# Feed-forward gate of a gated cross-attention block: product and maximum in one instruction, four buffers of gate integers

## The reference, cut to what matters

```
def act_qdq(x):                                  # one scale for the whole tensor
    scale = max(max(|x|) / 32767, 1e-12)
    return clip(round(x / scale), -32768, 32767) * scale
x    = act_qdq(layernorm(x))
up   = act_qdq(x @ Wup.T)                        # 2048 x 768
gate = act_qdq(x @ Wgate.T)                      # 2048 x 768
sig  = clip(round(sigmoid(gate) * 65536), 0, 65535) / 65536
gate = act_qdq(gate * sig)
o    = act_qdq(gate * up)
return o @ Wdown.T
```

## Time and profile before

| | us |
|---|---|
| median of 3 runs | 1151.55 (1150.32 to 1151.62) |
| the profiled execution | 1151.44 |
| its span in the trace | 1149.6 |
| DVE busy | 1006.2 (88%) |
| PE busy | 1075.3 (94%) |
| ACT busy | 604.5 (53%) |
| POOL busy | 37.0 (3%) |

### The profile page before, as it was taken

How to read it: one execution, slowest core, us unless ns; L and a number is a source line. 1 busy time by engine, 2 the same in 40 slices (tenths; PEclk the granted TensorE clock), 3 DMA queues, 4 the chain that set the end, 5 groups by cost and what they waited for, 6 DMA issues and landing times.

```text
span 1149.6 us, 20469 instructions
## 1 busy us (share of the span) xinstructions
PE 1075.3 (94%) x8342; PEld 501.4 (44%) x8342; DVE 1006.2 (88%) x1390; ACT 604.5 (53%) x706; POOL 37.0 (3%) x41
## 2 busy tenths in 40 slices
PE   5999999999999999999999999999999998999059
PEld 3443344434443444344434443444344323887049
DVE  7687988898989898999898989887999999749996
ACT  3555555555555555555555555554555464449652
POOL 0500000000000000000000000000000000003200
PEclk9999999999999999999999999999999999999579
DMA  8001300010001000100010001000000000000002
GB/s 264 18 20 25 120 20 20 20 38 20 20 20 37 20 20 20 38 20 19 21 38 20 20 20 38 20 20 20 30 20 19 20 29 10 1 1 1 0 0 74
DMA packets 37860, 34.57 MB, mean 30 GB/s; under 512 B 14209, under 2 KB 28738, under 8 KB 37510
## 3 DMA queue, kind: packets, MB, share of 16 engines
q1 hardware_dynamic: 37766, 33.26, 9.4%
HBM read 30.75 MB, written 2.36 MB: 29 GB/s over the span
## 4 chain that ended last, share of the span: by engine, by line
PE 80%; DVE 9%; ACT 5%; issue 5%; DMA 0%; POOL 0%; POOLq 0%; SPq 0%; DVEq 0%; ACTq 0%
PE ps L1384 26%; PE ps L1400 26%; PE ps L1247 5%; PE ps L1312 4%; PE ps L1257 4%; PE ps L1265 4%; PE ps L1534 3%; PE ps L1579 3%; DVE acc L925 2%; PE ps L1276 1%; DVE e_buf L1022 1%; DVE gt L1174 1%; ACT z L746 1%; ACT e_buf L664 1%; ACT z L748 1%
## 5 line engine op out<-in xcount | busy, mean ns | idle before, releaser
L664 ACT ACTIVATE e_buf<-ps 128x1024 f32<-128x1024 f32 x400 | 410.4, 1026 | 310.6 <-PE ps L1384 302.3
L1400 PE MATMUL ps<-e_buf,vb 64*64 64x512 f32 x3072 | 401.2, 593 | 4.7 <-DVE e_buf L1022 4.6
L925 DVE TENSOR_TENSOR acc<-acc,e_buf 128x1024 f32<-128x1024 f32 x318 | 387.8, 1220 | 0.0
L1022 DVE TENSOR_SCALAR e_buf<-e_buf 128x1024 f32<-128x1024 f32 x400 | 274.8, 687 | 53.9 <-ACT e_buf L664 52.6
L1384 PE MATMUL ps<-qb,kb_odd 64*64 64x512 f32 x1600 | 208.7, 589 | 0.0
L1384 PE MATMUL ps<-qb,kb_even 64*64 64x512 f32 x1600 | 208.6, 589 | 0.0
L1400 PEld LDWEIGHTS ps<-e_buf,vb 64*64 64x64 f32 x3072 | 111.7, 133 | 221.4 <-issue 187.4
L1384 PEld LDWEIGHTS ps<-qb,kb_odd 64*64 64x64 f32 x1600 | 61.5, 133 | 109.9 <-issue 109.6
L1384 PEld LDWEIGHTS ps<-qb,kb_even 64*64 64x64 f32 x1600 | 61.3, 133 | 110.2 <-issue 110.1
L1011 DVE TENSOR_TENSOR xacc<-ps,xacc 128x512 f32<-128x512 f32 x60 | 41.2, 690 | 35.4 <-PE ps L1312 34.9
L1534 PE MATMUL ps<-hT,wgu 128*128 128x512 f32 x288 | 67.7, 396 | 0.1
(11 more groups left out here) (151 smaller groups left out, 776.9 us busy)
## 6 DMA issues: line engine op xcount, KB each, us to landing
ebc<-el_rows SPq DMA_DIRECT2D x64, 128.0 KB, 2.9
rden<-inv_rows SPq DMA_DIRECT2D x62, 128.0 KB, 2.9
xacc<-in_x_dram SPq DMA_DIRECT2D x4, 512.0 KB, 7.2
wst<-in_L_xattn_Wkv_dram SPq DMA_DIRECT2D x16, 128.0 KB, 2.7
out_dram<-z SPq DMA_DIRECT2D x7, 256.0 KB, 2.5
wst<-in_L_xattn_Wq_dram SPq DMA_DIRECT2D x8, 128.0 KB, 2.7
wo_raw<-in_L_xattn_Wo_dram SPq DMA_DIRECT2D x8, 128.0 KB, 3.4
acc<-in_ctx_dram SPq DMA_DIRECT2D x2, 512.0 KB, 7.5
```

The lines of the kernel that those rows point to most:

```text
L664: nc.scalar.activation(e_buf[:, g % E_BUFS, :, :], sc[:, g % 2, :, :], ACT.Exp, scale=float(DH) ** -0.5).then_inc(exp_done, 1)
L925: dve.tensor_tensor(acc[:, t0 % 3, :, :], a, e_buf[:, tiles_to(t0, st) % E_BUFS, :, :], ALU.add).then_inc(summed, 1)
L1022: dve.tensor_scalar(tile, tile, EXP_LO, EXP_HI, ALU.max, ALU.min).then_inc(clip_done, 1)
L1400: ins = pe.matmul(ps_o[DH * h:DH * h + DH, half, :], vb[rows, p % 2, st, DH * h:DH * h + DH], e_buf[rows, g % E_BUFS, h, :], start=(st == ...
```

## The change

Each part by its line in the kernel before:

- The product (L1163) and its maximum (L809, `fst<-gt` in the product loop) become one instruction, `tensor_tensor_reduce`: it writes -(gi * su) over the chunk of `gt` and the largest of these values, with 0 as the start, to one column. The sign is turned, so the column holds the largest magnitude among the negative gates only. The last factor of the output (L1181) gets the sign back.
- The positive side comes from the largest gates, since x * sigmoid(x) grows with x there: DVE takes the plain maximum of each gate chunk (`gate_peak`, 12 reductions of 128 x 1024: ten in the gate phase, two between the first scale and the product loop). One column then goes through the same steps as the tensor: `peak_i` (DVE), sigmoid (ACT), `peak_u` (POOL), product (DVE in turn 2), all 128 x 1.
- `gi` has four buffers (`GI_BUFS`). In the product loop DVE makes eight of the twelve chunks of gate integers (0 and 1 ahead of the loop, 3, 4, 6, 7, 9 and 10 in it), ACT four (2, 5, 8, 11). ACT's order in a turn is now: sigmoid, two copies of up results, then perhaps `gi` of the next chunk.
- In the second product loop ACT's wait before `gi` is for the product four chunks back, not two.
- PE runs 12 matmuls on the identity, `keep_clock(7, 12)`, after the last up matmul.

The core of the diff:

```diff
@@ gpsimd, in the loop over su
+                if e == 1:
+                    pool.wait_ge(peak_sig, 1)
+                    pool.tensor_scalar(peak_u[:, :], peak[:, 1:2], U16, 1.0, ALU.mult, ALU.mult).then_inc(peak_su, 1)
@@ scalar
             for e in range(FCH):
-                f1_take(half + 2 * e)
-                f1_take(half + 2 * e + 1)
                 if e == 0:
                     act.wait_ge(scale_done, 2)
                     act.wait_ge(h_low, KT * NBS)
                 if e >= 2:
                     act.wait_ge(su_done, e - 1)
-                    act.wait_ge(gs_done, e - 1)
-
-                if e:
-                    nc.scalar.activation(gi[:, e % 2, :, :], chunk(gt, e), ACT.Copy, scale=fsc[:, 1, 2:3]).then_inc(gi_done, 1)
-                act.wait_ge(gi_done, e + 1)
-                nc.scalar.activation(sg[:, e % 2, :, :], gi[:, e % 2, :, :], ACT.Sigmoid, scale=fsc[:, 1, 1:2]).then_inc(sig_done, 1)
+                if gi_by_scalar(e):
+                    act.wait_ge(gi_scalar, e // 3 + 1)
+                else:
+                    act.wait_ge(gi_done, e - e // 3 + 1)
+                nc.scalar.activation(sg[:, e % 2, :, :], gi_at(e), ACT.Sigmoid, scale=fsc[:, 1, 1:2]).then_inc(sig_done, 1)
+                if e == 1:
+                    act.wait_ge(peak_gi, 1)
+                    nc.scalar.activation(peak[:, 1:2], peak_i[:, :], ACT.Sigmoid, scale=fsc[:, 1, 1:2]).then_inc(peak_sig, 1)
+                f1_take(half + 2 * e)
+                f1_take(half + 2 * e + 1)
+                if gi_by_scalar(e + 1) and e + 1 < FCH:
+                    if e + 1 >= GI_BUFS:
+                        act.wait_ge(gs_done, e + 2 - GI_BUFS)
+                    nc.scalar.activation(gi_at(e + 1), chunk(gt, e + 1), ACT.Copy,
+                                         scale=fsc[:, 1, 2:3]).then_inc(gi_scalar, 1)
             act.wait_ge(scale_done, 3)
             for e in range(FCH):
                 if e >= 2:
                     nc.scalar.activation(chunk(ui, e), chunk(up, e), ACT.Copy, scale=fsc[:, 2, 2:3]).then_inc(ui_done, 1)
-                    act.wait_ge(o_done, e - 1)
-                nc.scalar.activation(gi[:, e % 2, :, :], chunk(gt, e), ACT.Copy, scale=fsc[:, 3, 2:3]).then_inc(gq_done, 1)
+                if e >= GI_BUFS:
+                    act.wait_ge(o_done, e + 1 - GI_BUFS)
+                nc.scalar.activation(gi_at(e), chunk(gt, e), ACT.Copy, scale=fsc[:, 3, 2:3]).then_inc(gq_done, 1)
@@ vector
+            def gate_peak(e):
+                return dve.tensor_reduce(fst[:, 5, 2 * e:2 * e + 2], chunk(gt, e), AX_X, ALU.max)
+            def gate_integers(e):
+                if e >= GI_BUFS:
+                    dve.wait_ge(gs_done, e + 1 - GI_BUFS)
+                dve.tensor_scalar(gi_at(e), chunk(gt, e), fsc[:, 1, 2:3], None, ALU.mult).then_inc(gi_done, 1)
+            dve.memset(fst[:, 3, :], 0.0)
             for e in range(FCH):
                 ins = f1_top(0, e)
+                if 0 < e < FCH - 1:
+                    gate_peak(e - 1)
             link(ins)
             scale_of(1, 1, pieces, 1)
             link(dve.tensor_scalar(pre[:, 3:4], fsc[:, 1, 1:2], 1.0 / U16, None, ALU.mult))
-            dve.tensor_scalar(gi[:, 0, :, :], chunk(gt, 0), fsc[:, 1, 2:3], None, ALU.mult).then_inc(gi_done, 1)
+            gate_integers(0)
+            gate_integers(1)
+            gate_peak(FCH - 2)
+            link(gate_peak(FCH - 1))
+            link(dve.tensor_reduce(peak[:, 0:1], fst[:, 5, 0:pieces], AX_X, ALU.max))
+            dve.tensor_scalar(peak_i[:, :], peak[:, 0:1], fsc[:, 1, 2:3], None, ALU.mult).then_inc(peak_gi, 1)
             for e in range(FCH):
-                up_top = f1_top(1, e)
-                if e == FCH - 1:
-                    link(up_top)
-
                 dve.wait_ge(su_done, e + 1)
-                dve.tensor_tensor(chunk(gt, e), gi[:, e % 2, :, :], su[:, e % 2, :, :], ALU.mult).then_inc(gs_done, 1)
-                if e >= 1:
-                    dve.wait_ge(gs_done, e)
-                    top(fst[:, 3, 2 * e - 2:2 * e], chunk(gt, e - 1))
+                dve.tensor_tensor_reduce(chunk(gt, e), gi_at(e), su[:, e % 2, :, :], -1.0, 0.0, ALU.mult, ALU.max,
+                                         fst[:, 3, e:e + 1]).then_inc(gs_done, 1)
+                if e + 3 < FCH and not gi_by_scalar(e + 3):
+                    gate_integers(e + 3)
+                if e == 2:
+                    dve.wait_ge(peak_gi, 1)
+                    dve.wait_ge(peak_su, 1)
+                    dve.tensor_tensor(fst[:, 3, FCH:FCH + 1], peak_i[:, :], peak_u[:, :], ALU.mult)
+                ins = f1_top(1, e)
             dve.wait_ge(gs_done, FCH)
-            link(top(fst[:, 3, pieces - 2:pieces], chunk(gt, FCH - 1)))
+            link(ins)
@@ tensor, after the up matmuls
+            keep_clock(7, 12)
```

More of the change, by code:

```diff
@@ L60 @@
 GROUPS = NT // 2
+GI_BUFS = 4
 def rows_of(st):
@@ L232, in attention_ffn @@
         lnt = sb("lnt", [P, 4, LN3 + NT])
-        fst = sb("fst", [P, 5, 32])
+        fst = sb("fst", [P, 6, 32])
+        peak = sb("peak", [P, 2])
+        peak_i = sb("peak_i", [P, 1], I16)
+        peak_u = sb("peak_u", [P, 1], U16T)
         with ExitStack() as early:
@@ L282, in attention_ffn @@
             gt = sb("gt", [P, FT, N], stack=ffn)
+            gi_more = sb("gi_more", [P, 2, 2, NB], I16, stack=ffn)
             with ExitStack() as first:
@@ L326, in attention_ffn @@
         f1_ready, f1_out = sem("f1_ready"), sem("f1_out")
+        gi_scalar, peak_gi, peak_sig, peak_su = sem("gi_scalar"), sem("peak_gi"), sem("peak_sig"), sem("peak_su")
         gi_done, sig_done, su_done = sem("gi_done"), sem("sig_done"), sem("su_done")
@@ L372, in w_at, with gi_at, gi_by_scalar @@
             return wgu[:, m, part, :, :].rearrange("p k f -> p (k f)")[:, j * NB:(j + 1) * NB]
+        def gi_at(e):
+            return (gi, gi_more)[e % GI_BUFS // 2][:, e % 2, :, :]
+        def gi_by_scalar(e):
+            return e % 3 == 2
         def await_ui(eng, e):
@@ L1173, in _ @@
                 await_ui(dve, e)
-                dve.tensor_tensor(chunk(gt, e), gi[:, e % 2, :, :], chunk(ui, e), ALU.mult).then_inc(o_done, 1)
+                dve.tensor_tensor(chunk(gt, e), gi_at(e), chunk(ui, e), ALU.mult).then_inc(o_done, 1)
                 if e >= 1:
@@ L1180, in _ @@
             scale_of(4, 1, pieces, 3)
-            link(dve.tensor_tensor(fsc[:, 4, 3:4], fsc[:, 4, 1:2], tg[:, 1:2], ALU.mult))
+            link(dve.scalar_tensor_tensor(out=fsc[:, 4, 3:4], in0=fsc[:, 4, 1:2], scalar=-1.0, in1=tg[:, 1:2],
+                                          op0=ALU.mult, op1=ALU.mult))
             def out_integers(g, r0=0, r1=DM):
```

## The result

The changed kernel takes 1144.53 us (median of 4 runs, 1143.09 to 1145.30) against 1151.59 (4 runs): ratio 0.9939, 95% interval 0.9927 to 0.9952, so 7.1 us faster. The forecast was 1146.6, with 1142.7 to 1152.5 as its range.

What follows compares the result with a forecast made beforehand. DVE was taken to bound the first product loop, ACT close behind. With X = 1.38 the barrier's reduction comes 5.34 us earlier; less 0.4 for a stall, the gain is 4.9, giving 1146.6 us, range 1142.7 to 1152.5.

Steps and rivals of the forecast that it cites:

- The bound, and the two halves: First product loop: DVE's turn of 3.39 us is longest, ACT's 3.19 close behind; the change shortens both.
- the 0.2 that was reckoned: First product loop: shortening only one of DVE's and ACT's turns would gain 0.2 us a turn.
- X: First product loop, DVE: start distance behind a product with its maximum, taken as 1.38 us (1.13 + 0.06 + 0.19).
- PE and ACT were to set the end: Rival, end of first product loop: X near 1.13, no stall, 1142.7 us; the forecast's low end, no separate chance.
- Gate phase at nothing: Gate phase: ten added maxima on DVE cost 0, hidden behind PE in 1.58 us of idle time.
- The 0.45 left over: Gate phase: DVE's idle time between chunk maxima that remains after the added maximum, 0.45 us.
- Lead-in: From first scale to first product: 4.11 us summed, so the first product can start at 1036.31.
- The rival of half rate: Product with its maximum runs at half rate, X 2.44, loop 7.4 us later, 1159 us; chance 0.10.
- The stall on POOL: First product loop: one stall of at most 0.82 us until the order settles; 0.4 added.
- Port fight as a rival: First product loop: eleven products each wait up to 0.82 us for POOL's su, 1155.2 us; chance 0.14.
- Clock, second loop, sign: After the first product loop: low clock at the second scale, ACT's lead in the second loop and turned sign, each 0.
- The signs: Trace marks: product 1.45 to 1.5 us, barrier's reduction near 1071.2, su stretched towards 1.8 in most turns.

Runs made afterwards that it cites:

- e2: Changed kernel with gate integers as before (all but chunk 0 by ACT, two buffers, old order), keeping the product with its maximum and gate maxima: 1148.56 us.
- e3: Changed kernel with product and maximum apart again and no gate maxima; integers on DVE, four buffers and ACT's new order kept: 1155.72 us.
- e7: Changed kernel with each of the ten gate maxima in the gate phase done twice: 1150.23 us.
- e8: Changed kernel with products run alone on DVE behind its last result: f32 forms 1.22 to 1.23 us; bf16 plain 0.69, with maximum 1.22.
- e5: Changed kernel with POOL's sigmoid integers made twice for each chunk: 1152.13 us.
- e4: Changed kernel with DVE's integers behind the up maximum in every turn, not in front of it: 1145.21 us.
- e9: Changed kernel with DVE's integers of chunk 3 behind the up maximum of turn 0, and chunk 7's integers given to ACT: 1143.89 us.
- e10: Changed kernel with integers of chunks 3 and 4 behind the up maxima of turns 0 and 2, and chunk 7's given to ACT: 1144.47 us.
- e6: Changed kernel without the 12 matmuls on the identity and with the old wait (two products back) in the second product loop: 1144.48 us.

## Why the prediction was right, and where it was off

The forecast said 4.9 us and it was 7.1 by the medians, 6.79 in the loop.

- *The bound, and the two halves.* Right. DVE's turn ended last, ACT's 3.19 was next: e2 leaves ACT's turn and keeps a gain of 3 us (3.19 against 3.39 a turn, the 0.2 that was reckoned), e3 moves only the integers and loses. DVE stayed the bound (36.94 of 37.11) although X came out near the low end, close to which PE and ACT were to set the end. One slip without effect on the sum: ACT loses seven `gi`, not eight (eleven before, four after).
- *Gate phase at nothing.* Right, by the 33.40 us of both traces and by e7. The 0.45 left over is there in the trace.
- *Lead-in.* 4.11 us reckoned, 4.05 measured (1032.82 to 1036.87).
- *X, the start distance behind a product with its maximum.* The mis-sized term. I took 1.38, 1.13 with 0.06 for a second operation and 0.19 for the written column. It is 1.14: twelve times 0.24 is 2.9 us of gain that I did not count. The second operation costs nothing at this length (1226 against 1224 ns in e8, where the earlier trace rows had 748 against 691 at 512 columns, from other sources and with other neighbours), and the read-out runs beside the next instruction, where I had put it in the queue like an instruction of its own. The rival of half rate is refuted, by e8 for f32 sources and by this kernel for 16-bit integers. The Trainium skill, Vector Engine (DVE) Microarchitecture Reference, "Points that are easy to get wrong", has the shape that it calls `S2S2D2_STT` at half throughput with two SBUF sources other than bf16. The measurement decides against it here: the product with its maximum takes 1225 ns with both in the SBUF and 1220 with one in PSUM, and `SCALAR_TENSOR_TENSOR` 1226 with both in the SBUF. That the product with its maximum has this shape was taken for granted in the prediction; no run shows it.
- *The stall on POOL.* The second mis-sized term, with the other sign. I allowed one of at most 0.82 and took 0.4; there were two of 0.79, 1.57. I had the integers win over a waiting POOL from the start. In turns 0 and 1 POOL was there first, released by ACT's sigmoid while the product ran. The settling itself came as described, from turn 2 on. That the forecast came as near as it did is in part luck: these two errors have opposite signs. That the integers need the shared way too was only the page's word in the prediction; now 0.74 against 1.53 shows it, and the Trainium skill, Advanced Engine Details and Errata, "Mode Summary", agrees.
- *Port fight as a rival.* The mechanism is there (e5), but the changed kernel stays short of it, with 0.15 us to spare in a settled turn (1049.41 to 1049.56). e4, e9 and e10 show how easily it comes back.
- *Clock, second loop, sign.* All at 0, and so it was (e6 for the first two; the second loop has the same 29.30). The working for the clock was off all the same. The row has 24 matmuls and 2.84 us where 12 and 1.44 were reckoned, and the fall came 3.0 us after PE's last matmul (1064.96 to 1068.0), not 4.9; the two errors nearly cancel, and the fall at 1068.0 is luck. In e7 the clock was still at 1.00 when PE started again after 4.3 us. What sets this distance no run here shows, so 0 for the clock holds for the changed kernel and not for every variant.
- *The signs.* The product was to take 1.45 to 1.5 us and took 1.21, and the barrier's reduction was to start near 1071.2 and started at 1069.93, though this trace runs 0.62 late. `su` was to be stretched towards 1.8 us in most turns; from turn 2 on it is 1.41 in the turns where DVE makes integers and 1.05 in the others.

The sum: 12 x (1.14 - 1.38) = -2.88, stalls +1.17, lead-in -0.06, rest of the loop -0.08: 1.85 more than 4.94, which gives the 6.79.

Open is the difference of 0.3 us between the 6.79 of the stretch and the 7.06 of the medians; it is within the scatter of the runs, whose first scale ends up to 2 us apart from one trace to the next.

## What to carry to other kernels

When a maximum over a product can be had with one sign from the product's own instruction, take it there and get the other sign from a single column, where the product is known to grow with its input (here from the largest gates); but count first which engine is next, since here 3 of the 7 us came from the fusion and the other 4 only with work moved off the second engine (and its order and buffers changed). An engine that reads as fully busy may still be waiting: look for instructions of one shape with two durations. Where VectorE and GpSimd take turns on one way, the order that worked here is GpSimd released by the end of a VectorE instruction that needs it, with one behind it that doesn't; moving one instruction can shift the collision instead of removing it.

## What was not expected of the hardware

- A product with its running maximum costs a plain product's time (1.21 to 1.23 us for 128x1024), and its column's read-out 0.08 us beside the next instruction. Of the types tried, only bf16 shows a price: 1224 against 693 ns (e8).
- A stalled instruction need not be a large one. In e10 DVE's product of one column took 0.98 us instead of 0.15, beside POOL's `su`:

```profile
1040.53 1.57 POOL L562 TENSOR_SCALAR z<-z 128x1024 uint16<-128x1024 f32 x1 [0.70 <-ACT z L762]
1041.13 0.98 DVE L1209 TENSOR_TENSOR fst<-peak_i,peak_u 128x1 f32<-128x1 int16 x1
```
